# Order of two pieces of GpSimd work in the FFN tiles of an adaLN block: the multiply of the rounded x ahead of the LayerNorm scale and shift

## What is computed

```python
def fp4_quant_dequant(x):                 # blocks of 16 along the last axis
    scale = max(max(abs(xb)) / 6.0, 1e-12)
    idx = searchsorted(_MID, abs(xb / scale))
    return _GRID[idx] * sign(xb) * scale
def fp4_linear(x, w):
    return einsum('bsk,nk->bsn', fp4_quant_dequant(x), fp4_quant_dequant(w))
...
h = _layernorm(x) * (1 + ca) + sa
x = x + ga * attn(h, W_qkva, gamma)       # gated linear recurrence over 4096 steps
h = _layernorm(x) * (1 + cb) + sb
g = silu(fp4_linear(h, w_gate)) * fp4_linear(h, w_up)     # 512 -> 1408
x = x + gb * fp4_linear(g, w_down)                        # 1408 -> 512
```

## Time and profile before

| | us |
|---|---|
| median of 3 runs | 2070.73 |
| lowest and highest run | 2070.71, 2072.05 |
| span of the profiled execution | 2073.2 |
| own time of the profiled execution beside its span | none was listed; the span is used |
| TensorE busy | 1963.0 |
| VectorE busy | 1703.8 |
| GpSimd busy | 1106.1 |
| ScalarE busy | 619.0 |

### The profile page before, as it was taken

One profiled execution on the slowest core, in us unless ns is written; L12 is line 12 of the kernel. 1 busy time (PEld: TensorE's weight loads), 2 busy tenths in 40 slices (PEclk: granted clock), 3 DMA queues, 4 the chain that ended last, 5 costly groups with the idle time before them and its releaser, 6 DMA issues.

```text
span 2073.2 us, 27562 instructions
## 1 busy us (share of the span) xinstructions
PE 1963.0 (95%) x9401; PEld 930.4 (45%) x9401; DVE 1703.8 (82%) x2223; ACT 619.0 (30%) x878; POOL 1106.1 (53%) x1083
## 2 busy tenths in 40 slices
PE   4879999998999899999999999999999999999996
PEld 3334444444444444444444444444444444444442
DVE  3767776876866889889899898998988989989884
ACT  2224333333321232232322322223222232232321
POOL 2246464645532565665655656556565565565641
PEclk7989999999999999999999999999999999999998
DMA  7845646465552234343343333433434334333242
GB/s 253 279 105 148 167 143 169 141 154 144 150 133 87 64 75 97 68 89 82 70 100 68 81 89 68 98 75 78 94 68 91 80 70 100 68 85 86 68 93 48
DMA packets 417863, 219.20 MB, mean 106 GB/s; under 512 B 356214, under 2 KB 356226, under 8 KB 417804
## 3 DMA queue, kind: packets, MB, share of 16 engines
q1 hardware_dynamic: 417804, 218.44, 42.4%
HBM read 96.48 MB, written 33.57 MB: 63 GB/s over the span
## 4 chain that ended last, share of the span: by engine, by line
PE 44%; issue 15%; DVE 15%; DMA 9%; POOL 7%; SPq 7%; ACT 2%; DVEq 0%; ACTq 0%; POOLq 0%
PE bank L880 22%; PE bank L901 11%; PE bank L827 8%; DMA arena<-arena 6%; SPq L353 3%; SPq L410 3%; DVE arena L1213 2%; POOL arena L558 2%; POOL arena L576 2%; DVE arena L1173 1%; PE bank L793 1%; DVE arena L1180 1%; DVE arena L1060 1%; PE bank L852 1%; DVE arena L1135 1%
## 5 line engine op out<-in xcount | busy, mean ns | idle before, releaser
L880 PE MATMUL bank<-wgu_hi,arena 128*128 128x512 f16 (+1 forms) x3072 | 877.7, 362 | 23.6 <-DMA arena<-arena 22.6
L880 PE MATMUL bank<-wgu_lo,arena 128*128 128x512 f16 (+1 forms) x1536 | 556.1, 362 | 0.0
L827 PE MATMUL bank<-arena,wq_hi 128*128 128x512 f16 x1536 | 464.9, 385 | 17.1 <-DMA arena<-arena 8.1
L880 PEld LDWEIGHTS bank<-wgu_hi,arena 128*128 128x128 f16 x3072 | 300.9, 98 | 346.9 <-DVE arena L1180 26.6
L901 PE MATMUL bank<-wd_hi,arena 128*128 128x512 f16 x1408 | 431.3, 381 | 15.3 <-DMA arena<-arena 15.3
L827 PE MATMUL bank<-arena,wq_lo 128*128 128x512 f16 x768 | 295.1, 384 | 0.0
L901 PE MATMUL bank<-wd_lo,arena 128*128 128x512 f16 x704 | 267.9, 380 | 0.0
L584 POOL TENSOR_TENSOR arena<-arena,h_minus 128x1 f32<-128x1 f32 x64 | 97.9, 1529 | 317.4 <-DVE arena L1206 317.4
L827 PEld LDWEIGHTS bank<-arena,wq_hi 128*128 128x128 f16 x1536 | 151.5, 99 | 199.2 <-issue 19.8
L722 ACT ACTIVATE arena<-arena 128x1408 f32<-128x1408 f32 x64 | 88.2, 1378 | 501.3 <-DVE arena L1213 501.3
L901 PEld LDWEIGHTS bank<-wd_hi,arena 128*128 128x128 f16 x1408 | 138.3, 98 | 184.4 <-DMA arena<-arena 16.7
(11 more groups left out here) (132 smaller groups left out, 2696.3 us busy)
## 6 DMA issues: line engine op xcount, KB each, us to landing
arena<-in_L_attn_x_dram SPq DMA_DIRECT2D x32, 1024.0 KB, 6.6
arena<-x_scratch SPq DMA_DIRECT2D x128, 256.0 KB, 2.7
x_scratch<-arena SPq DMA_DIRECT2D x16, 1024.0 KB, 4.4
out_dram<-arena SPq DMA_DIRECT2D x64, 256.0 KB, 2.2
arena<-in_L_wmod_dram SPq DMA_DIRECT2D x6, 1024.0 KB, 8.8
arena<-in_L_attn_W_qkva_dram SPq DMA_DIRECT2D x1, 3072.0 KB, 15.0
wgu_hi<-in_L_ffn_w_gate_dram SPq DMA_DIRECT2D x1, 2816.0 KB, 13.9
wgu_lo<-in_L_ffn_w_up_dram SPq DMA_DIRECT2D x1, 2816.0 KB, 10.4
```

Of the source, the lines that this page charges most:

```text
L827: last = pe.matmul(dst[m % 2][:, :].rearrange("p (j t) -> p j t", j=NJ), w[:, k, at], uT[p][:, half, :, k, :], start=(n == 0), stop=(n == ...
L880: last = pe.matmul(dst[n][:, 0:w], xT[p][:, half, k, :], wt[:, k, cut], start=(m == 0), stop=(m == 3 * KD - 1))
```

## The change

In the list of one tile, GpSimd does `xq(i + 2)` ahead of `ffn_shifts(i + 3)`. Everything else keeps its order, on all engines.

```diff
@@ -607,11 +607,10 @@
 
                 def tile(i, p, b, first, last, b2, b3):
                     h_scales(i, p)
-                    if b3 is not None:
-                        ffn_shifts(i + 3, 1 - p)
                     if b2 is not None:
                         xq(i + 2, p, b2)
                     if b3 is not None:
+                        ffn_shifts(i + 3, 1 - p)
                         ffn_adaln(i + 3, 1 - p, b3)
                     if not (isinstance(i, int) and i < 1):
                         ffn_add_x(i - 1, 1 - p)
```

## The result

The changed kernel takes 2118.57 us (median of 4 runs, 2115.92 to 2123.39), the kernel before 2070.72 us (4 runs, 2068.06 to 2072.05). The ratio is 1.0235, with a 95% interval of 1.0212 to 1.0258: slower by 47.9 us, where 44.8 were forecast (2115.5 us).

The account below looks back on a forecast made before the run. A two-tile chain through GpSimd sets 21.73 us a tile, VectorE's 21.43 us loop just below. Delayed 1.03 us, VectorE's becomes 22.46: 1.0 + 43.8 = 44.8 us more, median 2115.5 us, range 2088 to 2134.

Parts of the forecast that it names:

- 1: L576 ends: GpSimd's multiply L576 no longer waits for the shifts and runs 4.0 us earlier, 1397.28 to 1398.34.
- Step 4: GpSimd's power L556, held up by L1234, pays up to 0.36 us extra and ends at 1401.86.
- the free power: Rival: L556 costs nothing extra after its hold-up; L1173 is 0.67 us late, 2094 us; chance 0.12.
- L554 slipping in ahead of L1229: Rival: GpSimd's L554 goes before VectorE's L1229 when L576 ends; L1173 0.40 us late, 2082 us; chance 0.05.
- Step 6: On ScalarE, L701 (`x_hi`) stands behind L688 (`ffn_apply`), which follows the shifts, so it starts 0.79 us later.
- step 7: GpSimd's L565 now waits for L688 and still holds up VectorE's L1173, which ends 1.03 us later.
- steps 3 to 5: GpSimd's L554 and L556 wait for VectorE's L1229 and L1234; L558, L560 take 0.19 us each; shifts end 1.39 us later.
- step 2: VectorE's L1229 meets the running L576 and takes 2.11 us; the 0.49 us are covered by its wait for L701.
- The faster rival: GpSimd's small operations are not held up behind L576; TensorE sets the tile, 2053 us or a little less; chance 0.08.

Follow-up runs that it names:

- the first experiment: Changed kernel with ScalarE doing x_hi, then ffn_apply, then h_hi, instead of ffn_apply ahead of x_hi: 2052.64 us, ratio 0.992 to the kernel before.
- the swap on VectorE: Changed kernel with VectorE doing gate_out (reads PSUM) ahead of h_quantised (both inputs in SBUF): 2117.97 us, ratio 1.0208 to the kernel before.
- the run with the small operation first: Kernel before with only the small multiply of the scales (L572) ahead of the shifts, L576 staying behind them: 2065.21 us, ratio 0.9979.

## Why the prediction was right

Point by point, in us from the start of `x_round`, by the written-out tile shown above:

| step | forecast | measured |
|---|---|---|
| 1: L576 ends | 1.89 | 1.86 |
| 2: L1229 takes; L1246 ends | 2.11; 5.66 | 2.11; 5.66 |
| 3: L554 ends | 3.40 | 3.39 |
| 4: L556 ends | 5.41 | 5.41 |
| 5: L560 ends | 5.95 | 5.95 |
| 6: L701 starts | 6.71 | 6.70 |
| 7: L1173 ends | 8.71 | 8.70 |
| tile | 22.46 | 22.45 |

Step 4 was the one without a row. The power does pay its extra length behind the hold: L556 took 1.94 us. Of its rivals, the free power would have shown 1.57 or so, and L554 slipping in ahead of L1229 would have shown 0.19; L554 has 1.57. Step 6 is confirmed by the first experiment, step 7 by L565's wait for `x_lo`, and the rule behind steps 3 to 5 by the swap on VectorE. L1229's 2.11 us of step 2 is the median of all 64 tiles. That VectorE's loop decides, and not the one over two tiles, shows in VectorE having stopped waiting for TensorE, as told above.

The faster rival named the right prize and the wrong obstacle. It asked whether the small operations are held up; they were, but the runs show that even with all of them held up the early multiply is worth having once ScalarE does `x_hi` ahead of `ffn_apply`.

Where I was off is the tile of the loop. Most tiles are not written out, and over all of them L565 gives (1987.3 - 904.8) / 48 = 22.55 us, 0.09 above the forecast. The rows of a looped tile show where most of it comes from:

```profile
1016.50 0.19 POOL L560 TENSOR_TENSOR arena<-arena,minus_one 128x1 f32<-128x1 f32 x1
...
1016.86 0.81 ACT L687 ACTIVATE arena<-arena 128x512 f32<-128x512 f32 x1 [7.87 <-POOL arena L560]
...
L565 POOL TENSOR_TENSOR arena<-arena,one_cb x49: 1268/1274/1287, 904.8 to 1987.3; 128x512 f32<-128x512 f32 x49
```

From L560's end to L687 it takes 0.17 us here and 0.03 in the written-out tile. It is so in every second looped tile; in the ones between it is 0.03 as well (L560 ends at 1039.29, L687 starts at 1039.32). The looped tiles last 22.54 and 22.59 us in turn, two of them 0.23 us more than two written-out ones. Of this 0.14 is the handing over. The other 0.09 stands on VectorE: in every second tile L1185 starts 1.39 us behind the first of the two L1179 ahead of it (999.44, 1000.83), otherwise 1.30 (1022.11, 1023.41). The kernel before has the 0.17 us in every second looped tile too (L560 ends at 923.20, L688 starts at 923.37). There L701 waited for the multiply and not for L688, so it cost nothing. I had read step 6's 0.04 us from a written-out tile alone.

The total is nearer than its parts, and that is luck. From the first L560 to the last one the changed kernel takes 2031.33 - 620.47 = 1410.86 us, the kernel before 1985.96 - 625.92 = 1360.04: 50.8 us more, where the sum had 44.8. From the last L560 to the end it takes 83.3 us instead of 87.2, where the forecast had put the last three tiles at nothing: TensorE was further on in its tile when that L560 started, and its part of the chain from there is 49.5 us instead of 52.1. Together (2114.6 - 620.5) - (2073.2 - 625.9) = 46.8 us, against 44.8 forecast. The spans alone differ by 41.4, because the first stage happened to be 5.4 us shorter. The step from the span to the median went the other way: the forecast took 2.5 us off, and the median came out 4.0 above the profiled span (2118.57, 2114.6).

## What to carry to other kernels

Moving work ahead on one engine wins only if the engine that uses it gets to it: here the result was ready 4 us sooner, and its user stood in ScalarE's list behind an operation that the same move had made later. So follow both moved pieces to their users and read the users' lists in order; changing the two lists together gave 1.2% where GpSimd's alone cost 2.3% and ScalarE's alone gave 0.6%. Where a loop runs over two tiles, a gain of x in its chain is worth about x / 2 a tile (0.20 of 0.41 us in one run, 0.12 of 0.31 in another), but a loss can meet an engine's own loop and be passed on for the greater part (here 0.72 of 1.02 us in a written-out tile).

## What the runs showed of the hardware

- A GpSimd operation that is issued while VectorE runs one with both inputs in SBUF waits for its end (seen with one element and with 512 per partition), and a VectorE operation of that kind waits for GpSimd's in the same way: L1172 took 1.35 us behind L565 and 0.69 without it. Beside an operation of VectorE that reads PSUM there is no wait (L556 0.55 us). The Trainium skill, "SBUF — State Buffer", section "SBUF: two separate sides", has the port pair taken for a whole instruction by whichever starts first; the rows agree, down to a one-element operation that is held up for 1.57 us.
- How long a held-up operation takes can be worked out from these rows: its wait, plus its own length when nothing holds it up, less 0.13 to 0.15 us. L1228 waits 0.62 us for L576 and takes 1.62 alone: 2.11 us. L1172 waits 0.79 us for L565 and takes 0.69 alone: 1.35. L554 waits 1.53 us for L1228 and takes 0.19 alone: 1.57. L556, the power, waits 1.53 us for L1233 and takes 0.55 alone: 1.94. So the one-element operations end 0.04 or 0.05 us behind VectorE's, and the power, by the same rule, 0.41 us behind.
- ScalarE took up L560's result after 0.17 us in every second looped tile, before and after the change, and after 0.03 or 0.04 us in all others. Why is open; no run took it apart.
- The first L560 came between 617.4 and 626.4 us in the profiled executions, though the first stage has the same code in all kernels. That could be a good part of the spread of the runs, and it is larger than the effect of the run with the small operation first. Its cause was not looked into.
